# Moving the exchanged rows of a chunked scan between SBUF partitions: one staging copy in DRAM with seven gathers, or 44 direct transfers

## What is computed

```python
alpha = jnp.exp(A * dt)
x_gamma = xh * lam[..., None]
x_beta = x_shift * ((1.0 - lam) * alpha)[..., None]
y = _ssd_chunked(x_gamma, A, B_mat, C_mat, dt) + _ssd_chunked(x_beta, A, B_shift, C_mat, dt)
y = _rms_norm(y.reshape(b, Tt, D_INNER)) * jax.nn.silu(z)
return y @ W_out
# inside _ssd_chunked, per chunk of 32:
Y_diag = jnp.einsum('bclhn,bcshn,bchls,bcshp->bclhp', Ch, Bh, Lm, xd)
h = h * dec[:, :, None, None] + s        # state carried over the chunks
```

## Time and profile before

| | |
|---|---|
| median of 3 runs | 2281.87 us (2273.9 to 2294.1) |
| the profiled execution | 2266.03 us, its span 2263.6 us |
| busy: PE, PE weight loads | 1892.4 us (84%), 1340.7 us (59%) |
| busy: DVE, POOL, ACT | 1363.3 us (60%), 823.4 us (36%), 760.0 us (34%) |
| PE's granted clock over the span | 0.931 of full |

### The profile page before, as it was taken

The page is one execution under the profiler, slowest core; times in us unless marked ns, Lnnn a source line. Parts: engine busy times, 40 slices in busy tenths (PEclk is TensorE's granted clock), DMA queues, the critical chain, the costliest instruction groups (busy, mean ns, idle before and its releaser), DMA issues. The chain is left out here.

```text
span 2263.6 us, 35897 instructions
## 1 busy us (share of the span) xinstructions
PE 1892.4 (84%) x9588; PEld 1340.7 (59%) x9589; DVE 1363.3 (60%) x3020; ACT 760.0 (34%) x1527; POOL 823.4 (36%) x823
## 2 busy tenths in 40 slices
PE   3698988979879889879889797746899999999990
PEld 2366756656657557557566575433566666666660
DVE  3777867867768767768677685322344444444445
ACT  3334423434334344334343342211233322223223
POOL 2124134134143142141341431222455555555554
PEclk7799999999999999989999998877999999999995
DMA  8123223123123033131231230019633333333337
GB/s 280 52 74 98 62 69 98 57 65 106 38 84 97 25 100 98 29 98 57 69 102 38 84 93 21 19 33 286 166 62 56 61 60 59 58 58 61 58 54 230
DMA packets 155390, 187.60 MB, mean 83 GB/s; under 512 B 38672, under 2 KB 134224, under 8 KB 154960
## 3 DMA queue, kind: packets, MB, share of 16 engines
q1 hardware_dynamic: 110288, 115.44, 16.2%
q0 software_dynamic: 40704, 67.40, 14.9%
q10 hardware_dynamic: 4352, 4.20, 0.5%
HBM read 119.23 MB, written 67.73 MB: 83 GB/s over the span
## 5 line engine op out<-in xcount | busy, mean ns | idle before, releaser
L1619 PE MATMUL pu<-w_ug,xh 128*128 x1728 | 360.5, 357 | 20.8 <-issue 11.9
L1758 POOL DMA_INDIRECT sums_dram<-yo,meta_in x144 | 228.0, 1583 | 253.0 <-DVE yo L1728 238.3
L1712 DVE TENSOR_TENSOR gate_hid<-pu,gate_hid 128x448 f32<-128x448 f32 x144 | 90.0, 625 | 360.3 <-ACT gate_hid L1680 356.6
L1619 PEld LDWEIGHTS pu<-w_ug,xh 128*128 128x128 bf16 x1728 | 168.7, 99 | 169.0 <-issue 45.4
L793 PE MATMUL pb<-x1T,w_sw 128*128 128x256 f32 x1024 | 231.1, 385 | 0.7 <-ACT x1T L911 0.7
L1680 ACT ACTIVATE gate_hid<-pu 128x448 f32<-128x448 f32 x144 | 78.3, 544 | 454.8 <-PE pu L1619 422.4
L793 PEld LDWEIGHTS pb<-x1T,w_sw 128*128 128x128 f32 x1024 | 196.0, 193 | 44.4 <-ACT x1T L911 10.8
L1645 PE MATMUL py<-w_dn,hh 112*128 x1728 | 215.2, 274 | 1.1 <-DVE yo L1728 1.1
L1645 PEld LDWEIGHTS py<-w_dn,hh 112*128 112x128 bf16 x1728 | 168.6, 98 | 22.3 <-issue 1.9
L999 POOL TENSOR_SCALAR yss<-yss 128x2 f32<-128x2 f32 x16 | 3.7, 232 | 459.2 <-ACT sq_a L898 459.2
L1748 POOL DMA_INDIRECT xin<-x_dram,meta_in x144 | 141.9, 986 | 74.5 <-issue 42.0
(11 more groups left out here) (246 smaller groups left out, 3565.4 us busy)
## 6 DMA issues: line engine op xcount, KB each, us to landing
w_stage<-in_w_ug SPq DMA_DIRECT2D x64, 224.0 KB
split_ug<-w_parts SPq DMA_DIRECT2D x64, 224.0 KB
w_ug<-split_ug SPq DMA_DIRECT2D x16, 896.0 KB, 13.9
xg_dram<-xg SPq DMA_DIRECT2D x16, 512.0 KB, 3.6
rows<-sums_dram SPq DMA_DIRECT2D x32, 256.0 KB, 5.5
w_stage<-in_w_dn SPq DMA_DIRECT2D x32, 224.0 KB
split_dn<-w_parts SPq DMA_DIRECT2D x32, 224.0 KB
w_dn<-split_dn SPq DMA_DIRECT2D x16, 448.0 KB, 14.8
```

Of the source, the lines that this page charges most:

```text
L1619: last = mm(pu[:, 2 * b + w, 0:EH], xh[:, b, xp, c, :], w_ug[:, bass.ds(e, 1), wp, c, w * EH:(w + 1) * EH], start=n == 0, stop=n == 3 * DC ...
L1712: vec.tensor_tensor(hid[:, m % 2, :], pu[:, 2 * (m % 2), 0:EH], gate, ALU.mult).then_inc(hid_ready.sem, 1)
L1758: nc.gpsimd.indirect_dma_start(out=sums_dram[m % 2], out_offset=bass.IndirectOffsetOnAxis(ap=meta[:, m, 0:1], axis=0), in_=yo[:, m % 2, :] ...
```

## The change

`xg_dram`, `store_xg` and `select` are gone. SP now copies the rows straight from `xg` to `xgs`, level by level (`select_halves`): for a block length q it issues, for each of the two tiles, q strided transfers or 128/2q contiguous ones, whichever is fewer. That makes 2, 2, 4, 4, 8, 8 and 16 transfers for the seven levels, 44 in a round, of 64, 64, 32, 32, 16, 16 and 8 rows of 2 KB. There are five semaphores in place of two: levels 0 and 1 of the order share one, then levels 2 and 3, and the last three have one each.

All five lists of `ORDER` are written anew. On SP the transfers stand between the weight pieces, and the first three levels are issued at the end of the round before; the lists of PE, ACT and DVE now begin in the middle of what was the end of a round (B6.1 and A2 of the neighbouring sequence), and D8 has moved on POOL from behind the gathers to between A5 and A6. Some signals are merged (`ang_ready` with `g_ready`, `qk_projected` with `v_projected`, `w_cumulated` with `v_cumulated`) with the same waits.

The core of the diff:

```diff
-EARLY = 4
+GROUP_OF = (0, 0, 1, 1, 2, 3, 4)
 ORDER = {
-    "SP": ("C7 A0 N0 A2 WL.0 WL.1 WL.2 WL.3 WL.4 WL.5"),
+    "SP": ("AX.3 AX.4 N0 AX.5 AX.6 C7 A0 WL.3- WL.4- WL.5- WL.0 WL.1 AX.0+ AX.1+ WL.2 AX.2+"),
-    "POOL": ("A6- A2 A2L AX.0 AX.1 D8+ B2 G1+ B3 A5 B6"),
+    "POOL": ("A2 A2L B6- B2 B3 G1+ A5 D8+ A6"),
...
-        xgs_in = [sig("xgs_in0", 16 * EARLY), sig("xgs_in1", 16 * (LV - EARLY))]
-        xg_stored = sig("xg_stored", 16)
+        xgs_in = [sig(f"xgs_in{n}", 16 * count) for n, count in enumerate((4, 8, 8, 8, 16))]
...
-            def store_xg(s):
-                sp.wait_ge(xg_ready.sem, xg_ready.at(s))
-                sp_carrier.take()
-                if later(s):
-                    for part in xgs_in:
-                        sp.wait_ge(part.sem, part.before(s))
-                        sp_carrier.take()
-                sp.dma_start(xg_dram.rearrange("(t p) d -> p t d", p=P), xg[:, :, :]).then_inc(xg_stored.sem, 16)
+            def select_halves(s, n):
+                if n == 0:
+                    sp.wait_ge(xg_ready.sem, xg_ready.at(s))
+                    sp_carrier.take()
+                    if later(s):
+                        sp.wait_ge(u_ready.sem, u_ready.before(s))
+                q = 2 ** LEVELS[n]
+                for t in range(NT):
+                    if 2 * q * q <= P:
+                        rows = [slice(t * q + i, P, 2 * q) for i in range(q)]
+                    else:
+                        rows = [slice(i * 2 * q + t * q, i * 2 * q + (t + 1) * q) for i in range(P // (2 * q))]
+                    for r in rows:
+                        sp.dma_start(xgs[r, n, :], xg[r, t, :]).then_inc(xgs_in[GROUP_OF[n]].sem, 16)
...
-            def select(s, part):
-                if part == 0:
-                    if isinstance(s, int) and s == 0:
-                        pool.wait_ge(setup_loaded.sem, setup_loaded.at(0))
-                    if later(s):
-                        pool.wait_ge(u_ready.sem, u_ready.before(s))
-                    pool.wait_ge(xg_stored.sem, xg_stored.at(s))
-                    carrier.take()
-                for k in LEVELS[:EARLY] if part == 0 else LEVELS[EARLY:]:
-                    nc.gpsimd.indirect_dma_start(
-                        out=xgs[:, k, :], out_offset=None, in_=xg_dram,
-                        in_offset=bass.IndirectOffsetOnAxis(ap=chosen_rows[:, k:k + 1], axis=0)
-                    ).then_inc(xgs_in[part].sem, 16)
...
             def decayed(s, n):
-                if n == 0:
-                    dve.wait_ge(xgs_in[0].sem, xgs_in[0].at(s))
-                elif n == EARLY:
-                    dve.wait_ge(xgs_in[1].sem, xgs_in[1].at(s))
+                if n < LV and n == GROUP_OF.index(GROUP_OF[n]):
+                    dve.wait_ge(xgs_in[GROUP_OF[n]].sem, xgs_in[GROUP_OF[n]].at(s))
```

More of the change, by code:

```diff
@@ L245, in build @@
         table = whole.enter_context(nc.sbuf_tensor("table", [1, 2, ntile], I32))
-        layers_block(nc, ins, nseq, cap, ntile, ident, waited, small, base, table, meta_dram, x3_dram, sums_dram, split_ug, split_dn, xg_dram)
+        layers_block(nc, ins, nseq, cap, ntile, ident, waited, small, base, table, meta_dram, x3_dram, sums_dram, split_ug, split_dn)
         experts_block(nc, ntok, cap, ntile, ident, waited, small, base, table, meta_dram, x3_dram, sums_dram, split_ug, split_dn)
@@ L272, in empty_slots, with layers_block @@
     return m.reshape(P, -1, 4)
-def layers_block(nc, ins, nseq, cap, ntile, ident, waited, small, base, table, meta_dram, x3_dram, sums_dram, split_ug, split_dn, xg_dram):
+def layers_block(nc, ins, nseq, cap, ntile, ident, waited, small, base, table, meta_dram, x3_dram, sums_dram, split_ug, split_dn):
     with ExitStack() as ctx:
@@ L441, in layers_block @@
         decay_ready = sig("decay_ready", 1)
-        ang_ready = sig("ang_ready", 1)
+        turned_ready = sig("turned_ready", 2)
         sin_ready = sig("sin_ready", 1)
-        g_ready = sig("g_ready", 1)
         roped = sig("roped", 1)
@@ L483, in layers_block @@
         x2n_ready = sig("x2n_ready", NT)
-        qk_projected = sig("qk_projected", NT)
-        v_projected = sig("v_projected", 1)
+        qkv_projected = sig("qkv_projected", 3)
         qk_ss_ready = sig("qk_ss_ready", NT * 2)
@@ L489, in layers_block @@
         wv_ready = sig("wv_ready", NT)
-        w_cumulated = sig("w_cumulated", 1)
-        v_cumulated = sig("v_cumulated", 1)
+        cumulated = sig("cumulated", 2)
         yc_ready = sig("yc_ready", 1)
@@ L672, in a3_late @@
                 pe.wait_ge(bcT_ready.sem, bcT_ready.at(s))
-                pe.wait_ge(g_ready.sem, g_ready.at(s))
+                pe.wait_ge(turned_ready.sem, turned_ready.at(s))
                 for t in range(NT):
@@ L759, in b3 @@
                               start=c == 0, stop=c == DC - 1)
-                last.then_inc(qk_projected.sem, 1)
+                last.then_inc(qkv_projected.sem, 1)
             def b3_v(s):
@@ L766, in b3_v @@
                                   start=c == 0, stop=c == DC - 1)
-                last.then_inc(v_projected.sem, 1)
+                last.then_inc(qkv_projected.sem, 1)
             def b4(s, part):
@@ L777, in b4 @@
                 last = mm(pb[:, 1 + part, D:2 * D], mat(ONES), wv[:, 0, part, :], start=False, stop=True)
-                last.then_inc((v_cumulated if part else w_cumulated).sem, 1)
+                last.then_inc(cumulated.sem, 1)
             def b5_first(s):
@@ L875, in a2_sin @@
             def a2_sin(s):
-                act.wait_ge(ang_ready.sem, ang_ready.at(s))
+                act.wait_ge(turned_ready.sem, turned_ready.at(s, 1))
                 act_f(cs[:, :, :, :], ang[:, :, :, :], ACT.Sin).then_inc(sin_ready.sem, 1)
@@ L928, in b3 @@
                 for t in range(NT):
-                    act.wait_ge(qk_projected.sem, qk_projected.at(s, t + 1))
+                    act.wait_ge(qkv_projected.sem, qkv_projected.at(s, t + 1))
                     for m in range(2):
@@ L1046, in a2 @@
             def a2(s):
-                pool.wait_ge(g_ready.sem, g_ready.at(s))
+                pool.wait_ge(turned_ready.sem, turned_ready.at(s))
                 pool.wait_ge(xs_ready.sem, xs_ready.at(s))
@@ L1088, in d8 @@
                             in_=meta[:, t, j, :], in_offset=None).then_inc(meta_stored.sem, 16)
-            run_skewed(pool, ORDER["POOL"], nseq, {"G1": g1, "A2": a2, "AX": select, "A2L": a2_late, "A5": a5, "A6": a6, "B2": b2, "B3": b3,
+            run_skewed(pool, ORDER["POOL"], nseq, {"G1": g1, "A2": a2, "A2L": a2_late, "A5": a5, "A6": a6, "B2": b2, "B3": b3,
                                                    "B6": b6, "D8": d8})
@@ L1178, in a2 @@
                 ca.step(vec.scalar_tensor_tensor(an, tu, -TWO_PI_LO, an, ALU.mult, ALU.add))
-                vec.tensor_scalar(an, an, 3.1415925, -3.1415925, ALU.min, ALU.max).then_inc(ang_ready.sem, 1)
+                vec.tensor_scalar(an, an, 3.1415925, -3.1415925, ALU.min, ALU.max).then_inc(turned_ready.sem, 1)
                 vec.tensor_tensor(g[:, :, :], ld[:, :, :], pa[:, 2, 0:2 * H].rearrange("p (t h) -> p t h", t=NT),
-                                  ALU.add).then_inc(g_ready.sem, 1)
+                                  ALU.add).then_inc(turned_ready.sem, 1)
             def a2_rope(s):
@@ L1237, in decayed @@
             def decayed(s, n):
-                if n == 0:
-                    dve.wait_ge(xgs_in[0].sem, xgs_in[0].at(s))
-                elif n == EARLY:
-                    dve.wait_ge(xgs_in[1].sem, xgs_in[1].at(s))
+                if n < LV and n == GROUP_OF.index(GROUP_OF[n]):
+                    dve.wait_ge(xgs_in[GROUP_OF[n]].sem, xgs_in[GROUP_OF[n]].at(s))
                 if n >= US:
                     dve.wait_ge(level_done.sem, level_done.at(s, n - US + 1))
-                src, by = (xgs[:, LEVELS[n], :], from_first[:, LEVELS[n], :]) if n < LV else (xg[:, 0, :], decay[:, LV, 0, :])
+                src, by = (xgs[:, n, :], from_first[:, LEVELS[n], :]) if n < LV else (xg[:, 0, :], decay[:, LV, 0, :])
                 vec.tensor_tensor(by_head(u[:, n % US, :]), by_head(src), spread(by, 2, HD), ALU.mult
@@ L1345, in b3 @@
             def b3(s):
-                dve.wait_ge(v_projected.sem, v_projected.at(s))
+                dve.wait_ge(qkv_projected.sem, qkv_projected.at(s))
                 for t in range(NT):
@@ L1916, in host_arrays @@
         "empty": empty_slots(x.shape[0]),
-        "halves": halves_of_levels(), "right": right_half(), "chosen_rows": (right_half() * P + np.arange(P)[:, None]).astype(np.uint32), "matrices": constant_matrices(), "small": small_constants(tile_count(x.shape[0])),
+        "halves": halves_of_levels(), "right": right_half(), "matrices": constant_matrices(), "small": small_constants(tile_count(x.shape[0])),
     }
```

10 lines of the change are left out of this document (4 added, 6 removed), and 16 rows, old and new, of the table ORDER.

## The result

The changed kernel takes 2214.74 us (median of 4 runs, 2207.39 to 2219.91), the kernel before 2277.89 (2270.55 to 2294.10): a ratio of 0.971 with a 95% interval of 0.965 to 0.977, 63 us less. The profiled execution takes 2207.39 us with a span of 2205.3; against the 2266.03 of before that is -58.6 us. It lies in three places. The `xg` product of sequence 2 starts at 182.02 us (186.22 before), the one of sequence 15 at 1280.92 (1333.09), and the rest of the span is 924.4 us (930.5): -4.2, -48.0 and -6.1 us.

What follows compares the result with a forecast made beforehand. PE was taken as nearest the limit, idling through its own late signals around the first feed-forward net. 2266 - 72 - 17 = 2177 us, plus half of the 15.8 us to the median, gave 2185; range 2140 to 2280.

Steps and rivals of the forecast that it cites:

- the likeliest case: Whole kernel: late signals mostly go and the new lists gain a little; 2145 to 2215 us, chance 0.53.
- upper bound of 85 us: Thirteen rounds of the sequence loop: most that could be saved if PE's late signals vanish, 6.56 us a round.
- The bound: Sequence loop: PE nearest the limit, idle about 11 us a round, 5.8 of it around the first feed-forward net.
- The gathers leave POOL: POOL in each round: without gathers and scatters back to back, PE's late signals go; -72 us.
- if remote waits move to where D8 now stands: Sign in the profile after: scatters alone cause the late signals, and the step blaming the pair fails; no size.
- The price of D8's new place: POOL between A5 and A6: A6 some 1 us late, 13 us in all, but hidden behind DVE's A2; 0 us.
- 44 transfers on SP: SP's direct copies each round: last level down 32.6 us after xg, needed at 40; 0 us, margin 7 us.
- the second rival: SP's transfers become the bound at AU.6 on DVE, making the kernel slower; about 2330 us, chance 0.14.
- the 88 of the prediction: SP's 44 transfers at the skill's 2 us each without overlap: 88 us, more than a round; rejected.
- The new lists: Reordered engine lists in each round: a quarter of PE's remaining 5.3 us idle time gained, 1.3 us; -17 us.
- The first round: First sequence: DVE's gather wait goes, weights queue behind transfers; A5 moves -6 to +8 us; counted as 0.
- The median's offset: Whole kernel: half of the 15.8 us from profiled run to median added back, the rest going with late signals.

Runs made afterwards that it cites:

- The old lists with D8 in the gap: Kernel before with only D8 moved in POOL's list, from behind the gathers to between B3 and A5, where POOL waits; 2165.01 us, ratio 0.950.
- D8 in the gap on both sides: D8 moved to where POOL idles: kernel before, between B3 and A5, 2165.01 us; changed kernel, between G1 and A5, 2154.54 us.

## Why the prediction was right, and which of its steps were not

2214.74 us lies in the range of 2140 to 2280 and 30 us above the 2185 forecast, at the upper edge of the likeliest case (2145 to 2215). If the two kinds of chip differ by the late signals alone, as far as these runs tell, they split the 63 us. Before: 2277.9 on late chips, 2169.3 on quiet ones, so 108.6 us of late signals (my upper bound of 85 us was for the thirteen rounds of a profiled execution 12 us below this median). After: 2214.7 and 2158.5, so 56.3 us. The change takes away 108.6 - 56.3 = 52.3 us of late signals, and 2169.3 - 2158.5 = 10.8 us by all the rest.

**The bound: right.** PE waited for consumers that its own late signals held, and these signals were what could be won. I took the best round seen less its one visible stall, 81.66 us. The old lists with D8 in the gap come to 1055.67 / 13 = 81.2 us a round, so that estimate was good.

**The gathers leave POOL, -72 us: right in mechanism, -52.3 measured.** The remote waits around the first net did vanish. The step that failed is the one that was to make D8's new place harmless: "So neither kind is enough by itself. Gathers and scatters back to back go with late signals of PE". The window of 1429 to 1441 holds eight scatters and a PE that is never idle, but one harmless place does not clear the scatters of every other, and a busy PE does not show that its signals are in time. Nor does the place alone settle it: around L647 the scatters held the signal in the twelve looped rounds and not in the one ahead of them, and the gathers alone did so in ten rounds of thirteen. Both windows of rows 8 lie outside the looped rounds. Between A5 and A6 the scatters delay L647's signal by 3.2 us or more in each looped round on a late chip; without them the delay is gone. The text named this outcome ("if remote waits move to where D8 now stands, the scatters alone are their cause"), and gave it no term and no chance.

**The price of D8's new place, 0: missed by 55 us, though the reasoning on POOL's queue held.** Of the ten microseconds of POOL I asked what stands behind them, and found nothing. The quiet chip shows that this is right: A6 starts 2.5 us late and the rounds take 80.3 us on average. The price is that of the late signal, 84.5 - 80.3 = 4.2 us a round. The windows split it. PE is busy for 1010.57 us in place of 984.22 (26 us, at a granted clock of 0.97 for 0.99) and idle for 1098.90 - 1010.57 = 88.3 in place of 59.7 (29 us). A stall of 2.5 us on DVE thus costs 1.7 times that, and nearly half of it goes with a lower granted clock. I had allowed 1 us a round. These are not further microseconds but the ones that remain above: 108.6 would have gone with nothing late, and 56.3 stayed.

**44 transfers on SP, 0: right, on half the margin.** Issues and one consumer, the changed kernel's round from 771.52:

```profile
773.65 2.46 SPq L594 DMA_DIRECT2D xgs<-xg  x4
...
783.81 10.44 SPq L594 DMA_DIRECT2D xgs<-xg  x16
...
794.98 14.68 SPq L594 DMA_DIRECT2D xgs<-xg  x24
```

```profile
815.63 0.68 DVE L1229 TENSOR_TENSOR u<-xgs,from_first 128x512 f32<-128x512 f32 x1
```

An issue takes 0.61 to 0.65 us and not 0.51, a landing 2.0 to 2.2 us and not 3.6 (the page has none for the 16 KB transfers). `xg` is done at 773.5. The last transfer is issued by 809.66 and, if it lands like the others, down 2 us later, 38.2 us after `xg` where I had 32.6; AU.6 reads it at 815.63, 42.2 us after `xg` where I had 40. The margin is 4 us where I had 7, and DVE never waits for `xgs`. The threshold at which SP would decide was put at 0.67 us per issue, so the second rival was nearer than I thought. What I called harmless behind SP's transfers, "none of them due for tens of us", holds only in the new lists: in the old ones the kernel with the transfers is 81 us slower, for the most part by the weight pieces behind them.

The Trainium skill, "DMA: Bandwidth & Descriptors", puts the fixed cost of a DMA near 2 us, in the section on the anatomy of one, which is about the DMAs that POOL issues, and says to coalesce small ones under "Rules for kernel authors". SP's landings of 2.0 to 2.2 us come to the same figure. The 44 issues take 27.6 us of SP a round, but the 2 us do not add up to the 88 of the prediction, since the transfers overlap.

**The new lists, -17 us: -10.8 measured**, on the quiet chips and with the new transfers in it. With D8 in the gap on both sides, on one late chip, the difference is 10.5 us (2165.0 and 2154.5), but there PE's waits behind the gathers' late signals (10.5 us in ten rounds) are in it. Of the 5.3 us a round that PE was idle in the best round I took a quarter as gained; 10.8 / 13 = 0.8 us, a sixth, came, and how much of that is the lists' alone no run tells.

**The first round, 0:** the A5 of the first sequence comes at 88.75 us for 90.84, and the `xg` product of sequence 2 at 182.02 for 186.22: -2.1 and -4.2 us, inside the -6 to +8.

**The median's offset, -8:** not there. The forecast fall from the median of 2281.87 was 72 + 17 + 8 = 97 us. The terms were too large by 19.7, 6.2 and 8 us, 33.9 together; the median of before itself came out 4.0 us lower with one more run, which leaves the 29.7 us between 2185 and 2214.7.

What stays open: what in the chip holds a signal of PE while POOL issues indirect DMAs, why two chips do it and two do not, why scatters in the gap hold nothing, and why the same burst at the same place held a signal in some rounds and not in others. No trace of the kernel before from a quiet chip was taken, and the eight scatters in their old place without gathers were not run on a late one.

## What to carry to other kernels

Before a large rewrite is costed, move the one suspect alone: one name in POOL's list brought 114 us here, and the change that moved it along with all five lists and the transfers brought 63. A window in which a suspect does no harm is evidence for that place and those rounds only; look at many rounds, and give "the trouble moves along with the suspect" a term and a chance in the sum. And compare a kernel with its predecessor on more than one chip, as a gain can be the cure of something that other chips do not have: 0.971 on the one kind, 0.9945 on the other.

## What was not expected of the hardware

- The same program takes 2273 to 2279 us on two chips and 2169 on two others (the kernel before), while another differs by 0.1% between them (2128.6 and 2126.3). In the changed kernel the traces show the difference as signals of PE that arrive late while POOL issues indirect DMAs: 3.2 us at L647 on the late chip, none on the quiet one. For the kernel before, of which no trace from a quiet chip was taken, it is inferred.
- On late chips gathers do it (2.8 us behind seven), scatters do it (3.2 us behind eight), fifteen in a row do it most (ACT held for 6 us and up to 10.3). They do not always do it: eight scatters in another place, 708.50 to 719.50, held nobody, and neither did those around L647 in the round ahead of the loop (258.94) or the gathers in three of thirteen rounds.
- A transfer between partitions of SBUF of 32 to 128 KB lands in 2.0 to 2.2 us and keeps SP for 0.61 to 0.65 us.
- Around the scatters in the gap the trace of a late chip lacks records of PE's signals, and the one of a quiet chip has them (the wait of 7.20 us before L911, the same on both). So a wait with the releaser "issue" can be an ordinary one.
